# One block of a vision network on one core: expert outputs copied out of PSUM by ScalarE, gated and added by GpSimd

## The reference, cut to what matters

```python
n = layernorm_over_channels(x)
value, query = dwconv3x3(n, w_v), dwconv3x3(n, w_q)        # stride 1
key, off     = dwconv3x3(n, w_k), dwconv3x3(n, w_off1)     # stride 2, 28 x 28
pos = tanh(gelu(layernorm(off)) @ w_off2 + ref_points)     # where to sample
v_s = bilinear_sample(value, pos)                          # 4 neighbours of each of 784 samples
out = (query^T key * 32**-0.5) v_s                         # per group of 32 channels, no softmax
x   = x + w_out @ out

t = layernorm_over_channels(x)                             # 3136 tokens of 96 channels per image
p = softmax(t @ gate_w + gate_b)                           # 4 experts, the best two kept, renormalised
y = sum_e p[e] * (gelu(t @ w1[e] + b1[e]) @ w2[e] + b2[e]) # 384 hidden channels per expert
x = x + y
```

## Time and profile before

| | |
|---|---|
| median of three runs | 856.83 us (855.06 to 860.57) |
| the profiled execution, its own time | 861.11 us |
| its span in the trace | 859.3 us |
| mean granted TensorE clock | 0.928 |
| instructions | 9579 |

### The profile page before, as it was taken

How to read it: one execution, slowest core, us unless ns; L and a number is a source line. 1 busy time by engine, 2 the same in 40 slices (tenths; PEclk the granted TensorE clock), 3 DMA queues, 4 the chain that set the end, 5 groups by cost and what they waited for, 6 DMA issues and landing times.

```text
span 859.3 us, 9579 instructions
## 1 busy us (share of the span) xinstructions
PE 737.2 (86%) x3186; PEld 511.9 (60%) x3186; DVE 617.6 (72%) x1511; ACT 385.6 (45%) x722; POOL 328.9 (38%) x185
## 2 busy tenths in 40 slices
PE   4988998559992999899992999899993997999996
PEld 4656565336761666566761666566661665688885
DVE  5669827797859568798859468899984244477775
ACT  2323222524551316444551316544540136599995
POOL 4002600016659501256659502245586111234443
PEclk9997979679995999999996999999996799999999
DMA  7023100011420100114421100111421000211111
GB/s 177 1 56 127 43 0 1 0 36 56 151 72 18 35 17 25 43 41 113 153 68 26 41 3 25 51 37 52 153 79 43 17 25 17 67 41 57 65 56 33
DMA packets 20258, 45.58 MB, mean 53 GB/s; under 512 B 4977, under 2 KB 9841, under 8 KB 19921
## 3 DMA queue, kind: packets, MB, share of 16 engines
q1 hardware_dynamic: 12480, 30.18, 11.4%
q10 hardware_dynamic: 4656, 9.96, 3.6%
q0 software_dynamic: 3072, 4.82, 2.3%
HBM read 30.30 MB, written 14.65 MB: 52 GB/s over the span
## 4 chain that ended last, share of the span: by engine, by line
PE 59%; DVE 19%; POOL 11%; ACT 4%; issue 4%; DMA 1%; ACTq 1%; POOLq 0%; DVEq 0%
PE py L668 12%; POOL big L1309 11%; PE pd L626 7%; PE ph L525 5%; DVE val L1023 4%; PE pa L477 3%; PE ph L684 3%; PE ph L685 3%; PE ph L686 3%; PE pa L617 2%; PE pd L595 2%; PE py L721 2%; PE ph L706 2%; PE py L718 2%; PE ph L708 2%
## 5 line engine op out<-in xcount | busy, mean ns | idle before, releaser
L1317 POOL TENSOR_TENSOR xbuf<-xbuf,ye 96x448 f32<-96x448 f32 x112 | 206.6, 1845 | 434.7 <-DVE ye L1238 432.8
L668 PE MATMUL py<-hid,w 128*96 128x448 f32 x504 | 238.3, 554 | 16.6 <-DVE ye L1238 8.7
L899 ACT ACTIVATE hid<-ph,b 128x448 f32<-128x448 f32 x252 | 159.0, 634 | 163.7 <-PE ph L686 147.9
L684 PE MATMUL ph<-x_hi,w_hi 96*128 96x448 f32 x252 | 166.1, 659 | 0.0
L1309 POOL DMA_INDIRECT big<-value_table,rows x64 | 113.7, 1776 | 83.4 <-DMA value_table<-valT 64.2
L1238 DVE SCALAR_TENSOR_TENSOR ye<-py,b,gate_all 96x448 f32<-96x448 f32 x112 | 75.3, 675 | 64.9 <-PE py L668 57.3
L668 PEld LDWEIGHTS py<-hid,w 128*96 128x96 f32 x504 | 82.3, 167 | 38.6 <-ACT hid L899 14.2
L685 PE MATMUL ph<-x_lo,w_hi 96*128 96x448 f32 x252 | 94.4, 375 | 0.0
L686 PE MATMUL ph<-x_hi,w_lo 96*128 96x448 f32 x252 | 93.8, 372 | 0.0
L1023 DVE SCALAR_TENSOR_TENSOR val<-xpad,conv_w,val 128x784 f32<-128x784 f32 x80 | 91.2, 1188 | 0.3
L1280 DVE TENSOR_TENSOR hid_lo<-hid,hid_hi 128x448 fp32r<-128x448 f32 x84 | 59.7, 710 | 27.3 <-ACT hid L908 27.2
(11 more groups left out here) (152 smaller groups left out, 1118.2 us busy)
## 6 DMA issues: line engine op xcount, KB each, us to landing
gate_all<-gate_rows SPq DMA_DIRECT2D x56, 336.0 KB
value_table<-valT ACTq DMA_DIRECT2D x8, 1176.0 KB, 7.6
out<-xbuf SPq DMA_DIRECT2D x28, 168.0 KB, 2.1
xbuf<-in_x SPq DMA_DIRECT2D x3, 1176.0 KB, 8.3
big<-value_table,rows POOLq DMA_INDIRECT x64
xbuf<-in_x SPq DMA_DIRECT2D x2, 336.0 KB, 5.1
query<-in_w SPq DMA_DIRECT2D x1, 576.0 KB
w<-in_w SPq DMA_DIRECT2D x1, 576.0 KB
```

What stands on the lines that cost most here:

```text
L668: nc.tensor.matmul(py[e % 2][0:C, 0:GPIX], w2[:, c, :], hid[:, k % 3, :], start=(j == 0), stop=(j == CPE - 1)).then_inc(hid_used, 1)
L684: nc.tensor.matmul(bank, w1_hi[:, cols], xh(b, g), start=True, stop=False)
L899: nc.scalar.activation(hid[:, k % 3, :], ph[k % 2][:, 0:GPIX], ACT.Gelu, bias=b1[:, k % NCH:k % NCH + 1]).then_inc(hid_act, 1)
L1317: ins = p.tensor_tensor(r, r, ye[0:C, e, :], ALU.add)
```

## The change

ScalarE copies the 84 outputs of the first three batches from PSUM into `ye`, adding b2 (an Identity activation with bias), in `gelus_to`, one chunk after an output's last one. GpSimd multiplies the slot in place with its gates and adds it to x, in two instructions. VectorE keeps only the 28 outputs of the last batch. The `turn` accounting is gone: VectorE's stages follow one another with nothing between. The gathers of the next batch are no longer issued in one go: with the ninth to twelfth output of a batch (the seventh to tenth in the last round) two of the eight tiles each, that is four of the 16 gathers, are issued between the output's multiplication and its addition. `ROUND` and `LAST_ROUND` have other numbers. There are still four slots `ye`: ScalarE's copy waits for the addition of the output four before (`added`).

```diff
-GATHER_AFTER = 2
+GATHER_AT = 8
+LAST_GATHER_AT = 6
+DEALT = 2
...
-FIRST_ROUND = [... ('exp', 2, 0, 0), ('gateT', 4, 0, 0), ('offc', 5, 0, 0), ('offs', 6, 0, 0), ...
-ROUND = [('valT', 28, 3, 19), ('xT', 33, 2, 0), ('keyT', 38, 0, 0), ('pad', 48, 3, 0), ('kv', 54, 0, 42), ('y', 57, 2, 3),
-         ('offT', 61, 0, 0), ('x1c', 64, 3, 24), ('exp', 71, 0, 0), ('gateT', 78, 0, 10.8), ('offc', 80, 0, 0), ('offs', 82, 0, 0),
-LAST_ROUND = [('valT', 26, 1, 19), ('keyT', 36, 0, 0), ('kv', 54, 0, 33), ('y', 56, 1, 3), ('x1c', 64, 3, 9.6), ('exp', 70, 0, 0),
-         ('gateT', 78, 0, 10), ('end', 84, 0, 1)]
+FIRST_ROUND = [... ('exp', 3, 0), ('gateT', 5, 0), ('offc', 5, 0), ('offs', 6, 0), ...
+ROUND = [('valT', 27, 3), ('xT', 33, 3), ('keyT', 38, 1), ('pad', 49, 3), ('kv', 52, 1), ('y', 55, 2),
+         ('offT', 61, 0), ('x1c', 66, 3), ('exp', 75, 0), ('gateT', 78, 0), ('offc', 78, 0), ('offs', 81, 0),
+LAST_ROUND = [('valT', 18, 0), ('keyT', 34, 1), ('kv', 60, 0), ('y', 60, 0), ('x1c', 66, 3), ('exp', 70, 0),
+         ('gateT', 79, 0), ('end', 84, 0)]
...
+        def gates_used(eng, number):
+            wait(eng, out_gated, min(number, DENSE))
+            wait(eng, last_gated, number - DENSE)
+        def bank_free(eng, number):
+            wait(eng, out_copied, min(number, DENSE))
+            wait(eng, last_gated, number - DENSE)
+        def added(eng, number):
+            wait(eng, out_added, min(number, DENSE))
+            wait(eng, last_added, number - DENSE)
...
-                    sp.wait_ge(ye_ready, FREE_OUTPUTS + b * OUTPUTS + EXPERTS * (g - 1) + 2 * k + 2)
+                    gates_used(sp, b * OUTPUTS + EXPERTS * (g - 1) + 2 * k + 2)
...
-                        pe.wait_ge(ye_ready, FREE_OUTPUTS + b * OUTPUTS + g * EXPERTS + e - 1)
+                        bank_free(pe, b * OUTPUTS + g * EXPERTS + e - 1)
...
+                def copy_output(n):
+                    g, e = n // EXPERTS, n % EXPERTS
+                    act.wait_ge(hid_used, b * CHUNKS + (n + 1) * CPE)
+                    added(act, b * OUTPUTS + n + 1 - EXPERTS)
+                    nc.scalar.activation(ye[0:C, e, :], py[e % 2][0:C, 0:GPIX], ACT.Identity, bias=b2[:, e:e + 1]).then_inc(out_copied, 1)
...
                         k = done[0]
+                        if k >= CPE + 1 and k % CPE == 1:
+                            copy_output(k // CPE - 1)
                         act.wait_ge(hid_full, b * CHUNKS + k + 1)
...
-                turn(0.0, back)
...
-                    turn(2.7)
                     query_tap(b, k)
...
-            def sum_group(b, g):
-                    pool.wait_ge(ye_ready, FREE_OUTPUTS + i * EXPERTS + e + 1)
-                    ins = p.tensor_tensor(r, r, ye[0:C, e, :], ALU.add)
-                    ins.then_inc(ye_summed, 1)
+            def add_group(b, g, beside):
+                r = x_of(b)[:, g * GPIX:(g + 1) * GPIX]
+                for e in range(EXPERTS):
+                    n = b * OUTPUTS + g * EXPERTS + e
+                    pool.wait_ge(out_copied, n + 1)
+                    if e % 2 == 0:
+                        pool.wait_ge(gate_in[e // 2], 16 * (b * NG + g + 1))
+                    p.tensor_tensor(ye[0:C, e, :], ye[0:C, e, :], gate_all[0:C, e, :], ALU.mult).then_inc(out_gated, 1)
+                    beside(e)
+                    pool.wait_ge(out_gated, n + 1)
+                    wait(pool, out_added, n)
+                    p.tensor_tensor(r, r, ye[0:C, e, :], ALU.add).then_inc(out_added, 1)
...
-            for b in range(BATCH):
-                for g in range(NG):
-                    sum_group(b, g)
-                    if g == GATHER_AFTER and b < BATCH - 1:
-                        gather(b + 1)
+            for b in range(BATCH - 1):
+                start = GATHER_AT if b < BATCH - 2 else LAST_GATHER_AT
+                for g in range(NG):
+                    add_group(b, g, lambda e: gather(b + 1, range(NS)[max(0, DEALT * (g * EXPERTS + e - start)):max(0, DEALT * (g * EXPERTS + e - start + 1))]))
+            for g in range(NG):
+                add_last_group(BATCH - 1, g)
```

More of the change, by code:

```diff
@@ L133, in at @@
         return self.start[name] + self.spread[name] * g // (NG - 1)
-    def last(self, name):
-        return self.start[name] + self.spread[name]
-    def needed(self, name):
-        return max(0, (self.start[name] + self.spread[name] - 2) // CPE - 1)
-    def outputs(self, name):
-        made = max(0, (self.start[name] - 1) // CPE)
-        number = max(self.needed(name), int((self.start[name] - 1) / CPE - OUTPUT_LAG), 0)
-        assert number <= made
-        return number
 FIRST_PLAN, PLAN, LAST_PLAN = Plan(FIRST_ROUND), Plan(ROUND), Plan(LAST_ROUND)
-for plan in (PLAN, LAST_PLAN):
-    assert EXPERTS * (GATHER_AFTER + 1) <= plan.outputs("kv")
-    assert plan.outputs("valT") < EXPERTS * (GATHER_AFTER + 2)
 def build(nc, t, out):
@@ L947, in link, with statistics @@
                 need(step(ins))
-            def statistics(np_, nt, eps, with_mean, turn):
+            def statistics(np_, nt, eps, with_mean):
                 S = lambda k: st[0:np_, 0:nt, k]
@@ L999, in norm_x, with norm_x1 @@
                         ins.then_inc(x_normed, 1)
[L1000 to L1004 removed]
+            def norm_x1(b, last):
+                norm_tokens(b, last, "x1c", LN2_EPS, x1_stats)
                 for g in range(0, NORM_DVE, 2):
@@ L1050, in normalise_off @@
                 link(last)
-                link(statistics(SP, NS, OFF_EPS, True, turn))
-                turn(3.0)
+                link(statistics(SP, NS, OFF_EPS, True))
                 for k in range(NS):
@@ L1242, in beside @@
-            def beside(plan, outputs_to):
-                stages = list(plan.dve_us)
-                at, spent = [0], [0.0]
-                def turn(us, name=None, upto=None):
-                    spent[0] += us
-                    if at[0] < len(stages):
-                        this = stages[at[0]]
-                        before = plan.outputs(stages[at[0] - 1]) if at[0] else 0
-                        late = 0 if at[0] else GATES_US
-                        part = min(1.0, max(0.0, spent[0] - late) / max(plan.dve_us[this] - late, 1.0))
-                        number = round(before + (plan.outputs(this) - before) * part)
-                        outputs_to(number if upto is None else min(number, (plan.at(*upto) - 1) // CPE))
-                    if name and name not in plan.dve_us:
-                        outputs_to(plan.needed(name))
-                    elif name:
-                        assert this == name, (this, name)
-                        outputs_to(plan.outputs(name))
-                        at[0] += 1
-                        spent[0] = 0.0
-                return turn
+                            raw_positions(b + 1)
@@ L1281, in last_experts @@
                     if k >= CPE + 1 and (k - 1) % CPE == 0:
-                        outputs_to((k - 1) // CPE)
-                outputs_to(OUTPUTS)
-            def no_turn(us, name=None, upto=None):
-                pass
+                        output(b, (k - 1) // CPE - 1)
+                output(b, OUTPUTS - 1)
             head(0)
-            rest(0, True, no_turn)
-            for b in range(1, BATCH - 1):
-                outputs_to = experts(b - 1)
-                rest(b, True, beside(PLAN, outputs_to))
-                outputs_to(OUTPUTS)
-            outputs_to = experts(BATCH - 2)
-            rest(BATCH - 1, False, beside(LAST_PLAN, outputs_to))
-            outputs_to(OUTPUTS)
+            for b in range(BATCH):
+                rest(b, b + 1 < BATCH)
             last_experts(BATCH - 1)
@@ L1302, in _, with gather @@
             p = nc.gpsimd
-            def gather(b):
-                pool.wait_ge(rows_ready, b + 1)
-                pool.wait_ge(table_out, 32 * (b + 1))
-                for k in range(NS):
+            def gather(b, tiles):
+                if 0 in tiles:
+                    pool.wait_ge(rows_ready, b + 1)
+                    pool.wait_ge(table_out, 32 * (b + 1))
+                for k in tiles:
                     for r in range(2):
```

116 lines of the change are left out of this document (43 added, 73 removed).

## The result

The changed kernel takes 888.20 us (median of four runs, 884.99 to 889.83) against 855.94 us before on the same chip (four runs, 854.53 to 860.57): 1.036 times as long, interval 1.031 to 1.041. The forecast was 846, its range 812 to 876. The profiled execution has a span of 888.0 us for 859.3. Some executions of a kernel are one or two per cent slower than its others; the ratios, and the medians of the kernel before in the experiments, leave them out.

What follows compares the result with a forecast made beforehand. TensorE, 86% busy, was taken as the fullest engine, with some 24 us a round standing still, mostly at the pads behind VectorE's query taps. -8.3 - 2 x 3 + 4 = -10.3 us gave 846 us, range 812 to 876.

Steps and rivals of the forecast that it cites:

- the one on the shared access: SBUF shared by VectorE and GpSimd: long tap runs shut GpSimd out; 18 val taps stay at 17.0 us.
- the price list: Part-by-part costs: VectorE loses 84 x 0.6 us, ScalarE gains 84 x 0.6, GpSimd 84 multiplications of 1.13 to 1.845.
- In total it fits: GpSimd: 84 added multiplications, 95 to 155 us, fit into 530 us of idleness; only when they run is open.
- the dangerous wait: ScalarE's copy waits for the addition four outputs back, held by a shut-out gather: +1.5 us a round, taken as -3.
- VectorE's 11.7 us idleness ahead of the taps goes: VectorE no longer waits for TensorE's outputs between statistics and query taps: 11.7 us; taps begin at 245.8.
- ScalarE's copies cost nothing: 84 copies out of PSUM of 0.6 us, 50 us in all, fit ScalarE's idle time; uncovered, up to 50 us.
- "-8.3" for the bank in the first round: TensorE's 8.3 us wait for an output bank VectorE has not emptied goes, as ScalarE copies at once: -8.3 us.
- The last round, "+4": Earlier val transposes, but gathers shut out in query taps delay TensorE: ends -14 and +9, +4 us taken.
- The sum: Whole kernel: -8.3 - 2 x 3 + 4 = -10.3 us, 850.8 on the profiled execution, 846 forecast.
- The Trainium skill's rule: SBUF port pair is locked for one whole instruction, so GpSimd would wait one tap, 0.95 us, not 21.
- rival A: GpSimd isn't held up by taps, so the stalls go: -55.5 us, 801, half of it 829; chance with half 0.25.
- Rival B: GpSimd becomes what everybody waits for, four slots full during val and key taps: 878 us; chance 0.25.

Runs made afterwards that it cites:

- e2: Changed kernel with all 84 GpSimd multiplications left out, a one-element memset in place of each; 854.67 us, 1.0024 of the kernel before.
- e5: Changed kernel without the multiplications of the first nine outputs of each of three batches (27 of 84); 869.64 us, 1.0236 of the kernel before.
- x1: Kernel before plus 84 ScalarE activations of the copies' shape, reading SBUF, for which TensorE's banks wait; 859.43 us against 857.03, ratio 1.0001.
- e3: Changed kernel plus a one-element VectorE memset after each query-tap instruction; 870.24 us, 1.0208 of the kernel before.
- e1: Changed kernel without the 48 gathers of batches 1 to 3; 859.24 us, 1.0036 of the kernel before.
- b1: Kernel before plus a one-element VectorE memset after each query-tap instruction; 856.31 us, 1.0046 of the kernel before.
- x2: Changed kernel with GpSimd's multiplications of each batch's first nine outputs replaced by in-place copies; 876.76 us, 1.0211 of the kernel before.

## Why the prediction was wrong

**The step that failed** is the one on the shared access: "Runs of 18 val taps (at 0.95 us, 17.0) ... remain", and with it the price list, which has no term for a multiplication that *does* get in among val taps. I read the taps as shutting GpSimd out, from the gather and the key taps, and so let the 84 multiplications cost GpSimd's time only ("In total it fits"). But rows of val taps said the opposite, and I had quoted them: "an addition that does get in stops VectorE: three taps take 4.47 instead of 2.84". In the middle round the seven multiplications are 7 x 0.89 = 6.2 us on VectorE, on the path to the val transposes (there are three in the first round's run and four in the last's). VectorE's small instructions, which the price list doesn't have either, add 3.4 us just ahead of the taps (7.6 for 4.2; 4.2 again in e2). e5 puts 18.6 us on the 27 multiplications of that part of the batches, e2 33.5 on all 84, and e2's VectorE is busy 43.3 us less. The second step that failed is a size, that of the dangerous wait, below.

Point by point:

- *VectorE's 11.7 us idleness ahead of the taps goes:* right. But the taps began at 253.4 and not at 245.8 as worked out. Val was late, and the four multiplications of the norm took 4.57 us (row above) where the earlier trace rows leave them 1.8.
- *ScalarE's copies cost nothing:* right; 0.629 us each for 0.6, and x1 shows no cost.
- *"-8.3" for the bank in the first round:* the bank's wait went, its gain did not. At 218.9 TensorE waits 11.7 us for val, nearly all in the place of the old 8.3. I had asked only what ends that wait, not what is late behind it.
- *The dangerous wait:* right in kind, place and size. Stop at the copy ahead of a gelu in the forties, behind a gather of 21.03 us, 23.3 us of TensorE. I took -3 us a round where I had worked out +1.5 for just this case; the gather's row stood in the trace, and the hopeful end was chosen against the nearest row. e3 prices it at 18 us, e1 at 29.
- *The last round, "+4":* +9.4, the end that I had given (+9). TensorE waits 9.7 us for val and 7.1 for a gelu; its victim is a multiplication, not a gather.
- *The sum* by rounds was -8.3 - 3 = -11.3 for the first, -3 for the second and +4 for the last, -10.3 in all. The rounds came out at +9.3, +11.8 and +9.4, head and tail at -1.8: +28.7.
- *The Trainium skill's rule* ("SBUF — State Buffer", "Who interferes with whom": the lock holds for one whole instruction) fits some runs of taps and not others. In the run of 18 val taps an addition takes 1.75 us, 0.6 more than alone, which is a wait for the tap under way: there it holds. In the run of six val taps (4.87 us) and in all unbroken runs of 21 query taps (20.2 to 22.2 us) it does not. My rival A, which followed from it, counted only GpSimd's side; that VectorE pays for each entry was missing there too.
- *Rival B* named the right engine and side, at 878 us, 10 short of the measured time; its mechanism, four slots full during val and key taps, did not occur: within the 29.5 us val run GpSimd idles before each multiplication, waiting for ScalarE's next copy. Copies waited for additions where the query taps run.

Open: what decides whether GpSimd gets in behind the tap under way or waits for the end of the run, since taps of one shape and operation do both; and why b1's memsets open nothing in its two full rounds.

## What to carry to other kernels

Before work is moved from VectorE to GpSimd, price it twice: the new instructions on GpSimd, and once more on VectorE wherever they fall beside its own. Here VectorE gave up an instruction of 0.675 us and paid 0.52 on average, and 0.89 among val taps, for its replacement on another engine. And never hold a buffer that others wait for across an instruction which a long run of another engine can shut out: look at what stands between taking the slot and giving it back.

## What the runs showed of the hardware

- In the runs of 18 val taps GpSimd and VectorE took turns: one tap longer by 0.89 us for each two-input instruction, by 0.34 for each copy, and GpSimd's additions there 1.75 for 1.14.
- VectorE's small instructions (98x16) beside GpSimd's took 1.00 and 1.07 us for 0.17 and 0.18 (e2). Without the 84 multiplications VectorE was busy 583.8 us for 627.1, with the same instructions.
- A run of 21 query taps back to back shut out a gather (21.03 us), a two-input multiplication (20.16 in e1) and, in x2's last round, a one-input copy that lasted 21.67 by the trace. A run of six val taps shut out a multiplication (4.87).
- With a one-element memset of VectorE between taps a gather got in each 1.9 us (e3), yet none in b1's two full rounds (21.76), where the 21 of a round had no measurable cost.
- In place and 96x448, GpSimd's one-input copy takes 0.55 us, its two-input multiplication 1.14.
